# Two transformer layers with sparse experts: index casts ahead of the row copies, later loads in attention, expert weights stored by partition

## The reference

```python
x = x + tanh(g_xattn[0]) * attention(layernorm(x), ctx, ctx)   # 32 query heads, 8 key/value heads, 16 wide
x = x + tanh(g_ffn[0]) * moe_0(layernorm(x), ...)   # 8 experts of width 256, 2 per token, and a shared one of 1024
x = x + tanh(g_xattn[1]) * attention(layernorm(x), ctx, ctx)
x = x + tanh(g_ffn[1]) * moe_1(layernorm(x), ...)   # 32 experts of width 192, 6 per token, and a shared one of 384
# an expert: (silu(t @ w_gate) * (t @ w_up)) @ w_down, summed over a token's experts with the router's weights
```

## Time and profile before

| stage (us from the start of the span) | what bounds it in the profile |
|---|---|
| 0 to 29, layer 0: loads, layer norm, first placements | PE works 3 us of 30 |
| 29 to 455, attention, 32 units | PE busy 396 us, DVE 370, ACT 277 of 425 |
| 455 to 800, router, sort, shared expert | PE |
| 800 to 1012, experts of layer 0, 37 tiles | PE busy 192 us of 212 |
| 1012 to 1465, the same attention in layer 1 | as above |
| 1465 to 1676, router, sort, shared expert | PE and DVE |
| 1676 to 2228, experts of layer 1, 111 tiles | PE busy 219 us of 240 from 1700 on; DMA engines 0.78 |

### The profile page before, as it was taken

One profiled execution on the slowest core, in us unless ns is written; L12 is line 12 of the kernel. 1 busy time (PEld: TensorE's weight loads), 2 busy tenths in 40 slices (PEclk: granted clock), 3 DMA queues, 4 the chain that ended last, 5 costly groups with the idle time before them and its releaser, 6 DMA issues. The chain is left out here.

```text
span 2227.7 us, 40122 instructions
## 1 busy us (share of the span) xinstructions
PE 1987.7 (89%) x10072; PEld 1224.0 (55%) x10073; DVE 1357.3 (61%) x2675; ACT 1087.7 (49%) x1673; POOL 723.2 (32%) x848
## 2 busy tenths in 40 slices
PE   4999999979999999993999999988888999899987
PEld 2343433334666757871334333334656887888776
DVE  5898988832234334434888988838774454444443
ACT  1666667732212225541666676742114565556554
POOL 3112111112101015553111121113753565555555
PEclk9999999989999999995999999989999999999998
DMA  5222222160000237765222222140026878777886
GB/s 176 62 54 60 61 56 66 29 227 0 1 1 1 95 109 172 156 106 176 54 67 54 58 60 58 41 150 0 1 83 160 179 178 191 170 188 177 187 179 106
DMA packets 130831, 219.88 MB, mean 99 GB/s; under 512 B 16930, under 2 KB 60964, under 8 KB 130724
## 3 DMA queue, kind: packets, MB, share of 16 engines
q1 hardware_dynamic: 96356, 138.80, 21.4%
q0 software_dynamic: 33792, 79.71, 18.4%
q10 hardware_dynamic: 576, 0.00, 0.0%
HBM read 114.64 MB, written 56.63 MB: 77 GB/s over the span
## 5 line engine op out<-in xcount | busy, mean ns | idle before, releaser
L568 DVE TENSOR_REDUCE maxima<-ring_ps 128x1 f32<-128x512 f32 x1024 | 648.4, 685 | 108.6 <-PE ring_ps L379 108.3
L465 ACT ACTIVATE probs<-score_ps 128x1024 f32<-128x1024 f32 x512 | 503.1, 1025 | 214.5 <-PE score_ps L396 212.5
L379 PE MATMUL ring_ps<-k_turned,q_turned 64*128 64x512 f32 x1024 | 412.8, 481 | 62.0 <-DMA q_turned<-q_lo 27.1
L379 PEld LDWEIGHTS ring_ps<-k_turned,q_turned 64*128 64x128 f32 x1024 | 176.7, 192 | 379.9 <-DVE maxima L568 224.2
L1072 PE MATMUL bank_f<-w_gu_parts_f,xg_T_f 128*128 x1800 | 370.7, 355 | 2.7 <-issue 2.7
L1072 PEld LDWEIGHTS bank_f<-w_gu_parts_f,xg_T_f 128*128 128x128 f32 x1800 | 329.9, 192 | 32.0 <-issue 4.1
L396 PE MATMUL score_ps<-q_turned,k_turned 64*128 64x512 f32 x1024 | 331.7, 444 | 12.3 <-ACT probs L465 12.3
L411 PE MATMUL out_ps<-probs,v_ones 128*32 128x512 f32 x2048 | 274.0, 607 | 1.7 <-ACT probs L465 1.6
L881 POOL DMA_INDIRECT xg_f<-xh_rows_f,idx_in_f x156 | 156.9, 1006 | 287.2 <-DVE idx_in_f L1523 193.3
L1097 PE MATMUL bank_f<-w_dn_parts_f,hg_T_f 96*128 (+1 forms) x888 | 246.7, 414 | 2.2 <-DVE hg_T_f L1629 1.4
L897 POOL DMA_INDIRECT out_x<-y_tok_f,idx_out_f x111 | 185.9, 1675 | 94.8 <-ACT y_tok_f L1271 45.4
(11 more groups left out here) (210 smaller groups left out, 2235.7 us busy)
## 6 DMA issues: line engine op xcount, KB each, us to landing
q_turned<-q_hi SPq DMA_DIRECT2D x128, 128.0 KB, 2.6
w_gu_f<-in_L_ffn_wg SPq DMA_DIRECT2D x32, 384.0 KB
w_gu_f<-in_L_ffn_wu SPq DMA_DIRECT2D x32, 384.0 KB
w_dn_f<-in_L_ffn_wd SPq DMA_DIRECT2D x32, 384.0 KB
k_turned<-k_hi SPq DMA_DIRECT2D x128, 64.0 KB, 2.1
q_turned<-no_max SPq DMA_DIRECT2D x64, 128.0 KB, 2.6
q_turned<-q_lo SPq DMA_DIRECT2D x64, 128.0 KB, 2.6
xh_rows_f<-xh_f SPq DMA_DIRECT2D x8, 1024.0 KB, 9.4
```

Of the source, the lines that this page charges most:

```text
L379: pe.matmul(ring(k, "max", i), q_turned[rows, slot, h // 2, c * P:(c + 1) * P], k_turned[rows, slot, :], start=True, stop=True).then_inc(m ...
L465: act.activation(probs[:, c % 2, pair, :, :], score_ps[:, pair, :, :], ACT.Exp, scale=float(D) ** -0.5).then_inc(exped, 1)
L568: dve.tensor_reduce(maxima[:, par, col:col + 1], ring(k, "max", i), AX.X, ALU.max).then_inc(max_taken, 1)
```

## The change

Three edits.

1. **Attention, SP and ACT.** The loads of x and of the turned keys `ctx_T` of batches 1 to 3 stood ahead of everything in SP's list. Now only batch 0 is loaded there; the two loads of batch 1, 2 and 3 are issued after the placements of unit 1, 3 and 5 of batch 0. ACT makes the high parts of their keys at units 2, 4 and 6 and no longer ahead of the first exponential.
2. **Expert weights.** The host lays them out so that a partition's weights of one expert are contiguous. In layer 1 a partition of gate and up is one run of 6144 bytes where it was eight runs of 768 (layer 0: one of 8192 where it was eight of 1024); of down one of 4096 where it was two of 2048. An expert takes two DMAs where it took three. The bytes are the same.
3. **Index column.** `rows_in` leaves `x_lo`. A new `next_rows(i + 4, half)` stands at the start of DVE's step i, ahead of `gu_lo`, and waits first until the gather of tile i + 2 has landed (it read the same column).

```diff
-            for b in range(B):
-                load_ctx_T(b)
-                if b == 0:
-                    sp.dma_start(ctx_tok[:], t["ctx"].rearrange("b (n p) d -> p (b n) d", p=P)).then_inc(ctx_loaded, 16)
-                else:
-                    load_x(b)
+            load_ctx_T(0)
+            sp.dma_start(ctx_tok[:], t["ctx"].rearrange("b (n p) d -> p (b n) d", p=P)).then_inc(ctx_loaded, 16)
...
                 place(b, k)
+                if b == 0 and k % 2 and k // 2 + 1 < B:
+                    load_x(k // 2 + 1)
+                    load_ctx_T(k // 2 + 1)
                 place_max(b, k)
...
             def step(b, k):
+                if b == 0 and k in (2, 4, 6):
+                    round_k(k // 2)
...
-            for b in range(1, B):
-                round_k(b)
...
             def load_expert(e, half):
-                sp.dma_start(w_gu[:, half, :, 0:F], t["wg"](e).rearrange("a (c p) f -> p (a c) f", p=P)).then_inc(expert_w, 16)
-                sp.dma_start(w_gu[:, half, :, F:2 * F], t["wu"](e).rearrange("a (c p) f -> p (a c) f", p=P)).then_inc(expert_w, 16)
-                sp.dma_start(w_dn[:, half, :, :], t["wd"](e).rearrange("a (c p) h -> p (a c) h", p=FW)).then_inc(expert_w, 16)
+                sp.dma_start(w_gu[:, half, :, :].rearrange("p c f -> p (c f)"), t["w_gu"](e).rearrange("a p n -> p (a n)")
+                             ).then_inc(expert_w, 16)
+                sp.dma_start(w_dn[:, half, :, :].rearrange("p c h -> p (c h)"), t["w_dn"](e).rearrange("a p n -> p (a n)")
+                             ).then_inc(expert_w, 16)
...
+            def next_rows(i, half):
+
+                dve.wait_ge(gathered[half], 16 * (i // 2) if isinstance(i, int) else 8 * i + (-8 * half))
+                rows_in(i, half)
+
             def x_lo(i, half):
                 dve.wait_ge(xg_hi, i + 1)
-                rows_in(i + 2, half)
...
             def step(i, half):
                 late = split_of(i - 1)
+                next_rows(i + 4, half)
                 with dve.If(late != 0):
                     gu_lo(late, 1)
                 times_up(i, half)
```

More of the change, by code:

```diff
@@ L784, in _ @@
                 if b == B - 1:
-                    sp.wait_ge(expert_w, 48)
+                    sp.wait_ge(expert_w, 32)
                     sp.wait_ge(hot_used, PAIRS)
@@ L795, in _ @@
                     e = pair * 2 + half
-                    sp.wait_ge(expert_w, 48 * e)
+                    sp.wait_ge(expert_w, 32 * e)
                     sp.nop(nofuse=True)
@@ L1228, in gu_hi @@
             def gu_hi(e, piece):
-                act.wait_ge(expert_w, 48 * e + 48)
+                act.wait_ge(expert_w, 32 * e + 32)
                 par = e % 2 if isinstance(e, int) else act.snap(e % 2)
@@ L1654, in _ @@
             turns = dve.value_load(turns_i[0:1, 0:1], min_val=4, max_val=64)
+            next_rows(2, 0)
             x_lo(0, 0)
+            next_rows(3, 1)
             x_lo(1, 1)
             times_up(0, 0)
+            next_rows(4, 0)
             x_lo(2, 0)
@@ L1662, in _ @@
             h_lo(0, 0)
+            next_rows(5, 1)
             x_lo(3, 1)
@@ L1676 @@
 INPUTS = ["x", "ctx_512", "g_xattn", "g_ffn",
-          "L0_ffn_w_gate", "L0_ffn_w_gate_up", "L0_ffn_w_down", "L0_ffn_w_sh_gate_up", "L0_ffn_w_sh_down",
-          "L1_ffn_gate_w", "L1_ffn_wg", "L1_ffn_wu", "L1_ffn_wd", "L1_ffn_sg", "L1_ffn_su", "L1_ffn_sd"]
+          "L0_ffn_w_gate", "L0_ffn_w_sh_gate_up", "L0_ffn_w_sh_down",
+          "L1_ffn_gate_w", "L1_ffn_sg", "L1_ffn_su", "L1_ffn_sd"]
 def build_program(nc, arg, out):
@@ L1753, with by_partition, flat @@
     laid_out["ctx_T"] = np.broadcast_to(turned, (2, KVH // 2, 2, D, TOK)).reshape(2, P, TOK).transpose(1, 0, 2)
+    def by_partition(w, rows):
+        e, n, f = w.shape
+        return w.reshape(e, n // rows, rows, f).transpose(0, 2, 1, 3)
+    def flat(w):
+        return w.reshape(w.shape[0], w.shape[1], -1)
+    laid_out["L0_w_gu"] = flat(by_partition(np.asarray(inputs["L0_ffn_w_gate_up"]), P))
+    laid_out["L1_w_gu"] = flat(np.concatenate([by_partition(np.asarray(inputs[f"L1_ffn_{n}"]), P) for n in ("wg", "wu")], axis=3))
+    laid_out["L0_w_dn"] = flat(by_partition(np.asarray(inputs["L0_ffn_w_down"]), 128))
+    laid_out["L1_w_dn"] = flat(by_partition(np.asarray(inputs["L1_ffn_wd"]), 96))
     for name, value in laid_out.items():
```

12 lines of the change are left out of this document (5 added, 7 removed).

## The result

The kernel after takes 2219.3 us (median of 4 runs, 2217.0 to 2222.8) against 2231.9 for the kernel before in the same comparison: ratio 0.9943, 95% interval 0.992 to 0.9965. It is 12.6 us faster where 36 were forecast. In a later comparison of 12 runs it took 2220.2, ratio 0.9959 (0.9939 to 0.9979). Its profiled execution took 2222.8, only 6.6 us less than that of the kernel before.

What follows compares the result with a forecast made beforehand. PE bounds attention and layer 1's experts, where late gathers behind expert loads cost about 40 us. Terms -28 - 3 - 5 = -36 us take the profiled 2229.35 to 2193; the median, 4.1 above, is 2197, range 2182 to 2217.

Steps and rivals of the forecast that it cites:

- The step that failed: Layer 1's experts: gathers starting 0.8 to 1.6 us earlier, about level with the load, take nearer 4 us than 7.
- 80%, 22 us: Layer 1's experts: 80% of 27.8 us of PE's waits for gathers would go, 22 us.
- the 5 us of clock: Layer 1's experts: fewer waits would end slow matmuls after them and the 0.97 clock, worth 5 us.
- A smaller error: Expert stage: after the change a gather waits only for its transpose plus 0.75 us, or POOL's previous scatter plus 0.30.
- only the shift: Rival, chance 0.24: gathers start earlier but DMA engines or scatters close in; layer 1's experts gain 12 us, total 2216.
- The load goes first: Rival, chance 0.06: in layer 1's experts gathers wait for the load in one piece, +20 us, 2253.
- The layout: Expert loads: same bytes in longer runs, 0 to 0.5 us cheaper per load, hidden on most tiles, inside the 28.
- Layer 0's experts: Layer 0's expert stage: 2.0 us of waits and a quicker first gather give -3 us, ends 0 and -5.
- the -28 for layer 1's experts: Layer 1's expert stage: shorter gather waits, clock and a quicker first gather give -28 us, ends -12 and -40.
- The new DVE wait: Expert stage: DVE's wait for the gather of tile i + 2 costs nothing, since PE waits for the same landing.
- Attention's starts: Attention's start: x of batch 1 lands 3.2 us earlier in layer 0, 1.9 in layer 1; -5 us, ends +5, -7.

Runs made afterwards that it cites:

- The cast ahead of the down split: The kernel after, with the next index column's cast moved to the end of DVE's previous step, before the down weights' low part: 2216.0 us, ratio 0.9929 to the kernel before.
- no load to speak of: The kernel after with 16 x 64 bytes copied in place of each expert load in the loop, results wrong: 2175.1 us, ratio 0.9753 to the kernel before.
- the down load late: The kernel after with down weights issued two 2.1 us pauses behind gate and up: 2186.8 us, ratio 0.9807; the same on the kernel before: 2195.1 us, 0.9834.
- One unit earlier: The kernel after with attention's loads for batches 1 to 3 behind placements of units 0, 2, 4: 2210.3 us, ratio 0.9909 to the kernel before.
- the kernel after with one pause: The kernel after, with SP copying 4 bytes and waiting about 2.1 us before each expert load in the loop: 2211.9 us, ratio 0.9921 to the kernel before.

## Why the prediction was wrong

**The step that failed** is the one that turned an earlier cast into an earlier landing: "Both then reach the engines about level with the load or before it, whose bytes do not move at once either. A gather so placed should take nearer 4 us than 7". The cast ahead of the down split puts the caught gathers 0.2 us behind the load's issue in the mean, 15 of 29 ahead of it (14 of these by at most 0.05 us), and they take 7.2 us. Both need some 1.8 us from issue to their first bytes, so level in issue is not ahead: 813 of the load's 1180 KB have started in the mean before the gather's first packet. With it falls the term "80%, 22 us" of waits and the 5 us of clock: waits went from 31.9 to 29.7 us and the clock stayed at 0.97.

What holds a caught gather is how many bytes are issued with the load. With the down weights 7 us away its last packet comes 1.3 us sooner (6.74 to 5.46), on the kernel before 1.4 (6.49 to 5.10), and with no load to speak of 3.29 us after issue. That the gain is alike in both layouts fits the bytes and not the number of runs: the down weights are a third of the bytes in both, but of an expert's runs they are 96 of 224 in the new one and 192 of 1216 in the old. So little suffices because the room is small: PE wants the rows two tiles of 4.35 us after its transpose, less the 0.63 that this takes, 8.1 us. In the kernel after the gather starts 1.5 us after the transpose, its last packet comes 6.74 later and PE follows 0.66 behind that (1766.61 to 1767.27), 8.9 in all; with the down load late it is 7.6.

Over the 29 caught gathers of the kernel after PE waits 26.5 us, 0.9 each, which is nearly all of the stage's 29.7; with the down load late it waits 0.7 us in all for such gathers. The 92 tiles go from 432.5 to 408.8 us: PE's idle time falls from 31.2 to 12.7, and its busy time from 400.4 to 394.8, with the clock at 1.00. The first 8 tiles give another 5.2. What is left of the 33 us lies outside this stage, where single profiles differ by 4 us or more. On the kernel before the 92 tiles go from 445.2 to 410.1.

**A smaller error stands in the same step.** "What remains before a gather is its transpose, plus 0.75 us." For most gathers that is so, 0.84 us. For the one that matters it is 1.5 in the rows above, since the cast stands behind `dn_lo`, whose end also releases the load. The order of DVE's step shows this without a run. Mending it (2216.0 against 2220.2, from two comparisons) is worth little.

**What the shift did give** is 12.7 us over 92 tiles (445.2 to 432.5). PE's waits for gathers are 4.8 us of it (30.6 to 25.8), its other idle time 3.2 and its busy time 4.6 (405.0 to 400.4). The caught gather's last packet came 8.01 us after the load and now 7.52; 27 x 0.5 = 13 would be the whole, but the waits did not fall by that much, so the agreement is chance. The size is also that of the rival "only the shift", -12 in this stage. Its reason was another one: neither the full DMA engines nor the scatter took over. The engines are busier with the down load late, 0.85, and the gathers are in time. ACT's waits at L1270 for a scatter's landing did not grow, they fell. They are here for the kernel before (1721 to 2153 us) and for the kernel after (1716 to 2148; us in total, times, longest):

```profile
ACT idx_out_f L1270 <- DMA out_x<-y_tok_f,idx_out_f: 31.7, 15, 3.9
```

```profile
ACT idx_out_f L1270 <- DMA out_x<-y_tok_f,idx_out_f: 5.7, 3, 3.4
```

**"The load goes first"** named what happens and mispriced it. It had the load's last piece added to every wait, +20 us, from 0.5 us behind the load's issue on. Most of the load was ahead of the gather already in the kernel before, with its three DMAs: 1007 of 1180 KB had started by the gather's first packet, against 1004 in the kernel after. So the change had little to add in the steady stage. Where it is right is the start of the stage. The Trainium skill, "DMA: Bandwidth & Descriptors", section "Queues, rings and completion order", has an engine drain a packet of some 9 to 17 descriptors from one queue before it turns to the next. The trace agrees in part: 0.8 us behind the load the first packet of a gather comes 4.20 us after its issue with 6 KB runs and 3.08 with 768-byte runs. 1.5 us behind it there is no such difference (4.24 for the layout alone, 4.26 for the kernel before). And the last packet comes at 6.74 and 6.76 all the same, which the rule alone does not say.

**The layout**, priced at 0 to 0.5 us a load and hidden, is a loss of 10.9 us alone and of nothing that the runs can tell beside the cast. The first 8 tiles of layer 1's stage show a part of it. They take 33.2 us in the kernel before, 33.1 with the cast alone, 34.5 without the layout; with it they take 39.9 (layout alone), 38.0 (no cast), 37.4 and 35.8 (the kernel after, twice). Later on it seems to pay some of that back beside the cast: 92 tiles take 437 and 439 us with the old layout, 432.5, 431.5 and 436.3 with the new, which is hardly more than profiles of the same code differ by. The packets show what could do it: the load is over sooner (7.2 us after its issue and not 8.9), and the gather behind the caught one (issued 4 to 5 us after the load) lands in 5.2 us with long runs and in 6.3 with short ones.

**Layer 0's experts**, -3 in the forecast, came out +4 (182.8 to 186.9 us from first to last transpose). Attention's edit alone, whose code there is that of the kernel before, shows 187.6, and the kernel without the layout 181.7. Single profiles of this stage differ by 4 us or more for no edit, so this term stays open. Of the -28 for layer 1's experts, -12.7 was seen past the first 8 tiles, and +4.2 in these.

**The new DVE wait**, costed at nothing, cost nothing that a run shows: the cast alone is no slower than the kernel before, and in the kernel after PE stands idle before its gate and up products (L1072) for 1.0 us in the whole stage.

**Attention's starts**, -5.1 in the forecast, are -2.4 and -0.8 in the profile and -3.1 in the run, within its interval. The mechanism was right, x sets the start, and so were both terms to about 1 us: x was issued at 24.25 (forecast 23.8) and took 6.2 us (forecast 5.8). In layer 0 the first transpose of the expert stage comes at 807.4 us in the mean of the five profiles with the old attention and at 805.0 in the eleven with the new, so the 2.4 us stand on more than one profile; layer 1 gains 0.5 by the same count.

What the forecast did not ask is how much x's landing still holds after the edit. One unit earlier gave another 10 us (2220.2 to 2210.3), and 7 to 9 beside the late down load. Of this the two profiles with that edit place 3.7 ahead of layer 0's experts and 2.4 between the two expert stages. So some 6 us are seen where the edit acts, and the rest is not placed.

## What to carry to other kernels

When a small transfer with a deadline is late beside a large one, do not race it to the queue: work out how many bytes are issued with the large one, and send these in pieces with the deadline transfer between them. Compare the lead that a race could give (here 1 us was needed) with the distance to the next such transfer, which will be caught in its place. First look whether what releases the large transfer is also what holds the small one back (here `dn_lo` held both), for then an edit moves them together. And price a move by the landing and not by the issue: the rows 1.2 and 0.6 us behind the load had the same landing.

## What the runs showed of the hardware

- A gather that POOL issues as SP issues a load of 1.18 MB, or up to 1.5 us behind it, has its last packet 7.3 to 8.2 us after the load's issue (means of the twelve profiles with the load issued whole); far from a load it needs 3.1 to 3.6 us in all, and so does one issued 1 us or more ahead of the load.
- The load itself has its last packet 7.2 us after its issue in runs of 6144 and 4096 bytes (the kernel after) and 8.9 us in runs of 768 and 2048 (the kernel after without the layout).
- A copy of 4 bytes on SP's queue takes longer behind a load. The pause issued 0.4 us behind gate and up ends at 1746.69, 4.3 us later, the second one after 2.7 (4.6 and 2.8 in the mean of 28 loads). Ahead of the load the same pause takes 3.0 us from its issue to the load's, as in the kernel after with one pause (start, us, engine and line, what):

```profile
1746.24 0.25 SPq L805 DMA_DIRECT2D pause_t_f<-in_L_ffn_gate_w  x1
...
1749.27 0.36 SPq L769 DMA_DIRECT2D w_gu_f<-in_L_w_gu  x1
```

- The granted clock of layer 1's expert stage, past its first 45 us, as a mean over the stretch, went with PE's waits for gathers: 0.97 to 0.99 in the kernels with 24 us of them or more in the stage, 1.00 in those with 12 or fewer, at the same work.
